# Attention and feed forward block on one core: the down product as three products of rounded and rest parts

## The reference

```python
# attention: group norm, q k v, softmax over 1024 keys for 8 heads of 16 channels, projection, residual
hid = group_norm(x); q, k, v = split(qkv_w @ hid + qkv_b)
x = x + proj_w @ (softmax(q.T @ k * scale) @ v) + proj_b
# convolution block, all 1x1
h = gelu(rmsnorm(x) * norm1_w);  x = x + conv_w @ h + conv_b
h = rmsnorm(x) * norm2_w
h = gelu(ffn_w1 @ h + ffn_b1)            # 128 -> 512 channels
x = x + ffn_w2 @ h + ffn_b2              # 512 -> 128 channels: the down product
```

## Time and profile before

| | us |
|---|---|
| median of three runs (lowest, highest) | 1763.99 (1761.72, 1764.31) |
| the profiled execution's own time | 1763.75 |
| its span | 1761.8 |
| second stage with all its parts, one image | 14.91 |
| same, image 14, which has no convolution beside it | 12.33 |
| TensorE busy in the span | 1698.3 |
| VectorE busy | 1492.8 |
| ScalarE busy | 1366.5 |
| GpSimd busy | 335.7 |

### The profile page before, as it was taken

One profiled execution on the slowest core, in us unless ns is written; L12 is line 12 of the kernel. 1 busy time (PEld: TensorE's weight loads), 2 busy tenths in 40 slices (PEclk: granted clock), 3 DMA queues, 4 the chain that ended last, 5 costly groups with the idle time before them and its releaser, 6 DMA issues.

```text
span 1761.8 us, 33312 instructions
## 1 busy us (share of the span) xinstructions
PE 1698.3 (96%) x12402; PEld 693.2 (39%) x12402; DVE 1492.8 (85%) x2606; ACT 1366.5 (78%) x2480; POOL 335.7 (19%) x411
## 2 busy tenths in 40 slices
PE   3999999999999999999999999999999997699999
PEld 2333333333333333333333333333333332355555
DVE  4899999999999999999999999999999992455552
ACT  1288888888888888888888888888888887466664
POOL 4101111111111111111111111111111011322220
PEclk8599999999999999999999999999999999799999
DMA  5422323232323132324242324141313011233341
GB/s 111 64 44 52 61 41 71 46 66 43 70 40 73 40 72 38 76 37 75 36 76 37 76 36 76 33 67 35 67 35 66 10 21 38 79 104 110 107 109 72
DMA packets 61121, 106.18 MB, mean 60 GB/s; under 512 B 27296, under 2 KB 30112, under 8 KB 60960
## 3 DMA queue, kind: packets, MB, share of 16 engines
q1 hardware_dynamic: 58656, 95.66, 27.6%
q10 hardware_dynamic: 2304, 8.39, 1.2%
HBM read 34.48 MB, written 9.06 MB: 25 GB/s over the span
## 4 chain that ended last, share of the span: by engine, by line
PE 83%; DVE 11%; issue 2%; SPq 1%; DMA 1%; POOL 1%; ACT 1%; DVEq 0%; ACTq 0%; POOLq 0%
PE psum L607 26%; PE psum L578 25%; PE psum L591 10%; DVE maxes L865 9%; PE psum L673 6%; PE psum L561 4%; PE psum L645 2%; PE psum L647 2%; PE psum L646 2%; PE psum L549 2%; PE psum L514 2%; PE psum L690 1%; DVE stats L881 1%; DVE rows L849 1%; SPq L309 0%
## 5 line engine op out<-in xcount | busy, mean ns | idle before, releaser
L865 DVE TENSOR_REDUCE maxes<-psum 128x1 f32<-128x512 f32 x2048 | 1269.5, 680 | 92.3 <-PE psum L578 90.8
L779 ACT ACTIVATE probs<-psum 128x512 f32<-128x512 f32 x2048 | 1107.4, 600 | 219.2 <-PE psum L591 196.6
L578 PE MATMUL psum<-k_stack,q_stack 62*128 62x512 f32 x2048 | 785.6, 461 | 19.0 <-DVE maxes L865 8.9
L591 PE MATMUL psum<-q_stack,k_stack 64*128 64x512 f32 x2048 | 770.8, 455 | 1.2 <-ACT probs L779 1.1
L607 PE MATMUL psum<-probs,values 128*32 128x256 f32 (+1 forms) x6912 | 621.2, 431 | 0.5 <-ACT probs L779 0.5
L578 PEld LDWEIGHTS psum<-k_stack,q_stack 62*128 62x128 f32 x2048 | 329.5, 188 | 561.8 <-DVE maxes L865 445.7
L591 PEld LDWEIGHTS psum<-q_stack,k_stack 64*128 64x128 f32 x2048 | 318.7, 185 | 14.8 <-ACT probs L779 10.5
L607 PEld LDWEIGHTS psum<-probs,values 128*32 128x32 f32 x6912 | 136.2, 108 | 286.8 <-issue 228.7
L673 PE MATMUL psum<-probs,inv_den 128*128 128x512 f32 x256 | 116.5, 598 | 0.0
L411 POOL CAST parts<-neg_max 128x16 fp32r<-128x16 f32 x64 | 12.6, 196 | 538.2 <-DVE neg_max L841 538.2
L788 ACT ACTIVATE probs<-psum,params_sb 128x512 f32<-128x512 f32 x128 | 82.5, 685 | 20.6 <-PE psum L647 14.2
(11 more groups left out here) (82 smaller groups left out, 1044.6 us busy)
## 6 DMA issues: line engine op xcount, KB each, us to landing
q_stack<-q_high SPq DMA_DIRECT2D x256, 64.0 KB, 2.2
k_stack<-k_high SPq DMA_DIRECT2D x128, 128.0 KB, 4.0
x_sb<-in_x SPq DMA_DIRECT2D x16, 512.0 KB, 5.2
q_stack<-q_low SPq DMA_DIRECT2D x128, 64.0 KB, 4.0
k_stack<-k_low SPq DMA_DIRECT2D x64, 128.0 KB, 4.3
attn<-raw SPq DMA_DIRECT2D x128, 64.0 KB, 2.3
inv_den<-inv_den_rows SPq DMA_DIRECT2D x128, 64.0 KB, 2.3
values<-inv_rms_rows SPq DMA_DIRECT2D x16, 512.0 KB, 5.0
```

The costliest lines, as they stand in the source:

```text
L578: nc.tensor.matmul(psum[:, BANKS + tile % BANKS, :], q_stack[used, place, chunk // 4, p, 128 * (chunk % 4):128 * (chunk % 4) + 128], k_sta ...
L591: nc.tensor.matmul(psum[:, tile % BANKS, :], k_stack[used, place, p, 128 * chunk:128 * chunk + 128], q_stack[used, place, t, p, :], start= ...
L779: nc.scalar.activation(probs[:, tile % 8, :], psum[:, tile % BANKS, :], ACT.Exp, scale=SCALE).then_inc(probs_ready, 1)
L865: nc.vector.tensor_reduce(maxes[:, chunk // 4, j, 4 * p + chunk % 4, key_half:key_half + 1], psum[:, BANKS + max_tile(u, s, k) % BANKS, :] ...
```

## The change

`down` no longer multiplies float32 operands. It uses rounded and rest parts of the second weight (`w2_high`, `w2_low`, made once, in the other halves of `q_high` and `q_low`) and of the gelu's output (`act2_high`, `act2_low`, in `k_stack`, which the attention has finished with), in three matmuls per block. GpSimd makes all eight rounded parts of an image and, for the last block of each half, the rest part too (`round_hidden`); VectorE makes the other six rest parts (`low_hidden`). TensorE does `hidden(c, 1)` ahead of `down(c, 0)`. The down product of the second half goes to another bank, which it shares with the second half of the convolution. ScalarE takes the copy of the sums from VectorE, from call 0 on.

```diff
+        w2_high, w2_low = q_high[:, HIDDEN:2 * HIDDEN], q_low[:, HIDDEN:2 * HIDDEN]
+        def act2_high(t, m):
+            return k_stack[:, m, 0, HALF * t:HALF * t + HALF]
+        def act2_low(t, m):
+            return k_stack[:, m, 1, HALF * t:HALF * t + HALF]
-        HIDDEN_BANKS, CONV_BANKS, SUMS_BANK, OUT_BANK = (0, 1, 2, 7), (3, 4), 5, 6
+        HIDDEN_BANKS, CONV_BANKS, SUMS_BANK, OUT_BANKS = (0, 1, 2, 7), (3, 4), 5, (6, 4)
# GpSimd
+            def round_hidden(c, t):
+                at_least(pool, ffn_ready, (c - 1) * NT + (t + 1))
+                for m in range(HB):
+                    pool.wait_ge(act2_ready, c * (NT * HB) + (t * HB + m + 1))
+                    nc.gpsimd.tensor_copy(act2_high(t, m), act2(t, m)).then_inc(act2_rounded, 1)
+                pool.wait_ge(act2_rounded, (c * NT + t + 1) * HB)
+                nc.gpsimd.tensor_tensor(out=act2_low(t, HB - 1), in0=act2(t, HB - 1),
+                                        in1=act2_high(t, HB - 1).bitcast(fp32), op=ALU.subtract).then_inc(act2_third, 1)
             def refine(c):
+                if has_image(c):
+                    round_hidden(c, 0)
+                    round_hidden(c, 1)
                 if norms(c):
# TensorE, convolve
                 if t == 0:
                     pe.wait_ge(act1_split, c + 1)
+                else:
+                    at_least(pe, result_ready, (c - CONV) * NT)
# TensorE, down
-                at_least(pe, result_ready, c * NT + t)
+                at_least(pe, result_ready, (c - 1) * NT + (t + 1))
+                if t == 1:
+                    at_least(pe, conv_taken, min(c + CONV + 1, IMAGES) * NT)
                 for m in range(HB):
-                    pe.wait_ge(act2_ready, c * (NT * HB) + (t * HB + m + 1))
-                    at = HIDDEN + 128 * m
-                    mm = nc.tensor.matmul(psum[:, OUT_BANK, :], w12[:, at:at + 128], act2(t, m),
-                                          start=(m == 0), stop=(m == HB - 1))
+                    if m < HB - 1:
+                        pe.wait_ge(act2_split, (c * NT + t) * (HB - 1) + m + 1)
+                    else:
+                        pe.wait_ge(act2_third, c * NT + t + 1)
+                    features = slice(128 * m, 128 * m + 128)
+                    out = psum[:, OUT_BANKS[t], :]
+                    nc.tensor.matmul(out, w2_high[:, features], act2_high(t, m), start=(m == 0), stop=False)
+                    nc.tensor.matmul(out, w2_high[:, features], act2_low(t, m), start=False, stop=False)
+                    mm = nc.tensor.matmul(out, w2_low[:, features], act2_high(t, m), start=False, stop=(m == HB - 1))
# TensorE, refine
+                    hidden(c, 1)
                     down(c, 0)
-                    hidden(c, 1)
                     down(c, 1)
# ScalarE, gelu_hidden
-                    if m == 0:
-                        at_least(act, ffn_ready, c * NT + (t - 1))
+                    if m < HB - 1:
+                        at_least(act, act2_split, ((c - 1) * NT + t) * (HB - 1) + m + 1)
+                    else:
+                        at_least(act, act2_third, (c - 1) * NT + t + 1)
# ScalarE, refine
                     gelu_hidden(c, 0)
+                    if norms(c):
+                        act.wait_ge(sums_ready, c + (FIRST + 1))
+                        at_least(act, rms_in_done, c * 64 + 64 * FIRST)
+                        nc.scalar.copy(sums, psum[:, SUMS_BANK, :]).then_inc(sums_taken, 1)
+                    gelu_hidden(c, 1)
                 if has_image(c + FIRST - 1) and not is_first(c + FIRST - 1):
                     activate(c)
-                if has_image(c):
-                    gelu_hidden(c, 1)
# VectorE, refine
-                if norms(c):
+                if has_image(c):
+                    low_hidden(c, 0)
+                if norms(c) and c < 0:
                     dve.wait_ge(sums_ready, c + (FIRST + 1))
...
+                if has_image(c):
+                    low_hidden(c, 1)
                 if has_image(c + CONV - 1):
...
-                    split_weights(2, w12[:, 0:HIDDEN], w1_high, w1_low)
+                    split_weights(2, w12, q_high[:, :], q_low[:, :])
+            def low_hidden(c, t):
+                for m in range(HB - 1):
+                    dve.wait_ge(act2_rounded, (c * NT + t) * HB + m + 1)
+                    nc.vector.tensor_tensor(out=act2_low(t, m), in0=act2(t, m), in1=act2_high(t, m).bitcast(fp32),
+                                            op=ALU.subtract).then_inc(act2_split, 1)
```

More of the change, by code:

```diff
@@ L235, in build @@
             sem("act1_rounded"), sem("act1_split"), sem("normed2_rounded"), sem("normed2_split"))
+        act2_rounded, act2_split, act2_third = sem("act2_rounded"), sem("act2_split"), sem("act2_third")
         conv_ready, conv_taken, hidden_ready, act2_ready, ffn_ready, result_ready, result_out = (
@@ L982, in output_half @@
                     at_least(dve, result_out, c * 16)
-                nc.vector.scalar_tensor_tensor(out=result[:, HALF * t:HALF * t + HALF], in0=psum[:, OUT_BANK, :],
+                nc.vector.scalar_tensor_tensor(out=result[:, HALF * t:HALF * t + HALF], in0=psum[:, OUT_BANKS[t], :],
                                                scalar=params[:, FFN_B2:FFN_B2 + 1], in1=image_of_x(c, HALF * t, HALF),
```

## The result

The changed kernel takes 1832.12 us (median of 4 runs, 1829.56 to 1833.3) against 1763.63 before: a ratio of 1.0388, 95% interval 1.037 to 1.0406. It is 68.5 us slower. The forecast was 1819.5 in a range from 1764 to 1850.

What follows compares the result with a forecast made beforehand. TensorE alone set the pace before; afterwards GpSimd's and VectorE's turns were to lengthen each image. 52 + 1.7 + 2.1 - 0.5 + 0.5 = 55.8 us on 1763.75 gave 1819.5 us, range 1764 to 1850.

Steps and rivals of the forecast that it cites:

- The step on which it rested: Second stage: a GpSimd cast or difference keeps VectorE out likewise, for its duration less 0.15 us; exclusion both ways had 0.57.
- What it took from the rows of before: Earlier trace: beside VectorE's two-input L929, GpSimd's L491 took 1.23 us instead of 0.22, power L494 3.94 instead of 2.91.
- One image, step by step: Second stage, from the convolution's second half: GpSimd and VectorE take turns, making an image 18.9 us, 4.0 more than 14.91.
- The 13 images that have all parts: Calls 0 to 12 of the second stage, each 4.0 us longer, together 52 us.
- the last three: Images 13, 14 and 15, which lack some parts: +1.7, +2.1 and -0.5 us.
- the start: Before the first image, the second weight's split doubles from 512 to 1024 columns: some 0.8 us, given 0.5.
- a case of its own at 1845 to 1875 us: Rival called clock in the prediction: 1845 to 1875 us, chance 0.10.
- signs named for a right forecast: Second stage: GpSimd casts of 0.61 to 1.2 us, L1021 0.69 to 1.3 or up to 1.9, images 18 to 20, clock 1.00.
- The new wait: The convolution's second half needs the second down product's bank, so it starts after the last `output_half`, at 18.85 us.
- Only GpSimd is held up: Rival: VectorE's instructions keep their times, an image takes 0.1 to 1.9 us more, 1766 to 1791 us; chance 0.18.
- Faster: Rival: GpSimd's casts and VectorE's differences interleave at next to no cost, an image 14.7 us, 1757 us in all; chance 0.12.
- No change: Rival: exclusion eats what the three products give, 15.0 to 15.1 us an image, 1760 to 1767 us; chance 0.03.

## Why the prediction was right, and where it was off

**The step on which it rested** held. The choice was that GpSimd's casts and differences keep VectorE out as VectorE's keep GpSimd out, each for its duration less 0.15 us. A pair of cast and difference takes 1.0 us from one to the next; 0.46 + 0.54 gave 1.00. Taking GpSimd's reading away undid the turns, and so did taking away VectorE's second input.

**What it took from the rows of before.** That L491 pays beside two SBUF inputs and not beside one, and that the power's 16 columns are no longer held up when L974 starts 2.36 us behind it, shows in another call of that trace:

```profile
1623.32 0.74 DVE L983 SCALAR_TENSOR_TENSOR attn<-psum,params_sb,x_sb 128x512 f32<-128x512 f32 x1
1623.48 0.22 POOL L491 TENSOR_TENSOR mean_eps<-rms_in,eps 128x16 f32<-128x16 f32 x1 [10.23 <-DMA rms_in<-values]
1623.78 2.91 POOL L494 TENSOR_TENSOR rms_out<-mean_eps,neg_halves 128x16 f32<-128x16 f32 x1
1623.98 1.22 DVE L929 TENSOR_TENSOR q_stack<-k_low,q_stack 128x1024 fp32r<-128x1024 f32 x1
```

L491 keeps its 0.22 in the middle of L983, which has one tensor input in SBUF. L929 starts 0.20 us behind the power, and neither is held up: 1.22 and 2.91, where 0.04 ahead of the power it made it 3.94. So 0.20 us after its start neither the power nor VectorE was held any more, and the row of L974 could say nothing of casts of 512 columns, beside which VectorE's differences took 1.09 us (median of L1021) in place of 0.69.

**One image, step by step.** Counted from the convolution's second half at 1623.33, the worked turns and the measured ones are: GpSimd's first difference released at 8.15, ended at 8.44; the last cast of the second half at 12.2, ended at 12.59; GpSimd's second difference 13.9, ended 14.27; second norm ended 15.1, measured 15.35; next second half of the convolution at 18.9, measured 19.00. The order guessed (GpSimd's difference ahead of the second norm) is the one that occurred.

**The sum.** It was 55.8 us over the profiled execution of before; the spans of the two profiled executions, 1830.1 and 1761.8, stand 68.3 apart. The 13 images that have all parts were put at 52 and took 59.4 us more; the last three were put at 3.3 and took 6.8, the start at 0.5 and took 2.1. Of the start's 2.1 us, 1.9 stand there before any changed instruction has run (the first square of the stage begins at 1498.59 against 1496.68), and are scatter of the first stage.

The 13 are off by the clock: 19.0 us was right for an image at full clock, but the mean is 19.6. The prediction gave the clock a tenth, as a case of its own at 1845 to 1875 us. No run shows that case; in its place the runs show a cost beside the turns: nine of the 13 images took 19.4 to 20.1 us, the other four 19.1 to 19.2, and it cost 0.6 us an image, 7.5 in all. **The term that was mis-sized is this one**: the forecast put it at nothing, although it left TensorE busy for only 13.43 us of 18.9, and the earlier trace rows had a stretch with TensorE busy for 15.88 us of 36 at a granted clock of 0.57. There is a little luck in the 52: the image of call 0 took 16.19 us before and not 14.91, so a step from 14.91 to 19.0 in all 13 would have given 53, and at full clock it was 51.9.

The last three are the other term. Between last `output_half`s, images 13, 14 and 15 took 17.40, 15.62 and 13.83 us, against 14.91, 12.33 and 12.34 before: 2.5, 3.3 and 1.5 more, where 1.7, 2.1 and -0.5 were put. With the clock held up by fills they took 17.41, 15.11 and 13.51, so 0.8 of this is the clock and the rest is turns and waits counted too low, most of all in image 15; in which of its steps was not looked into. With the three differences, 7.4, 3.5 and 1.6, added, the forecast gives 1832.0.

Two of the signs named for a right forecast did not come either: casts reach 1.61 us where 1.2 was the most, since some wait for a norm, and the clock is 0.91 and not 1.00.

**The new wait** at the bank was named at its place. The prediction made it the end of the chain, and it is (0.82 us). With it gone an image at full clock is only 0.5 us shorter, so VectorE's order holds most of the time without it.

**The rivals.** "Only GpSimd is held up" is gone: VectorE's L1021 and its norms are longer by the other's time. "Faster" gave 1757 us for a kernel without exclusion; the run with memsets, which is nearly that kernel, took 1749.86, with 14.13 us an image where 14.7 had been worked out. "No change" is out: the interval of the ratio begins at 1.037.

**What was not tried**: the whole change with ScalarE rounding, or with only the second half on GpSimd; what each turn costs by itself if VectorE issues ahead of GpSimd in every one; and whether another order of VectorE's instructions would let the second half's turns fit as well.

## What to carry to other kernels

Before work goes to an engine that has time to spare, ask what it reads and beside whom: two idle shares do not add up if the two engines take turns at reading SBUF, and here 7.5 us of GpSimd work and 3.5 us of VectorE work became some 10 and 7. Such turns cost next to nothing while they fit under the engine that sets the pace, and lengthen the image once they lie on the chain that it waits for: half of the change gained 0.6% with the rounding on ScalarE and 0.5% with it on GpSimd, where the whole of it on GpSimd lost 3.9%. So change a part first, and see whether the bound engine stays busy. And where a forecast puts gaps into a TensorE that was busy throughout, price its lower clock in the forecast itself: here it read 0.91 over the steady part and cost 7.5 us of the 59.4.

## What the hardware showed that was not expected

An added wait can cost through the clock: moving a bank, worth 0.5 us in an image at full clock and so 6.5 in the 13, saved 10.8 in them. Filling the gap with matmuls whose result nobody needs made the 13 images of the changed kernel 7.5 us faster (granted clock 0.91 to 1.00).

What a VectorE instruction with two SBUF inputs does to the 16-column power hangs on 0.2 us. With the first half on ScalarE the second norm starts 0.24 us before the power, with it on GpSimd 0.23, and in both the power takes 3.81 us in place of 2.91. In the changed kernel L964 starts 0.43 us behind the power (1639.27 and 1638.84), and both keep their plain times, 1.21 and 2.91, as L929 did at 0.20 us behind it in the kernel before. The rows with ScalarE rounding:

```profile
1604.95 1.28 DVE L995 SCALAR_TENSOR_TENSOR q_full<-x_sb,params_sb,raw 128x1024 f32<-128x1024 f32 x1
1604.33 0.78 POOL L499 TENSOR_TENSOR mean_eps<-rms_in,eps 128x16 f32<-128x16 f32 x1 [9.58 <-DMA rms_in<-values]
1605.19 3.81 POOL L502 TENSOR_TENSOR rms_out<-mean_eps,neg_halves 128x16 f32<-128x16 f32 x1
```
